# Attention score stages: the last value group at full width, and a reordering of eviction, transposition and stores

## The chip, the cores and the metric

The kernel runs on one NeuronCore of a Trainium2 chip, in one launch. The metric is the device time of a run in microseconds (us); lower is better.

## The reference

Three layers work on x of 2 x 1024 x 128 floats: a mixture-of-experts attention layer added with weight 0.5, a causal multi-query attention layer, and the first layer again. The change touches only the first and the third, which are the same code (phase 0 and phase 1). Cut to what matters, for each batch:

```python
h = layernorm(x)                                   # 1024 tokens, 128 channels
q, k, v = (moe_proj(h, W, b) for W, b in ...)      # gated mix of 4 experts; 16 heads of 8
scores = einsum('bthd,bshd->bhts', q, k) / sqrt(8)
attn = softmax(scores, axis=-1)                    # not causal, all 1024 x 1024
out = einsum('bhts,bshd->bthd', attn, v).reshape(B, T, C)
x = x + 0.5 * (out @ Wo + bo)
```

## The kernel before

**Units.** A unit is one head of one batch; each phase has 32 of them. `it` counts groups of four units and `g` (0 to 3) is the place in the group. The engines run in their own instruction order and meet at semaphores. First iterations and last ones are written out, the middle ones are hardware loops.

**Two score computations.** Softmax needs each query's maximum before the exponentials. For a unit, TensorE computes all scores twice. `max_tile` (L1151) computes 128 queries x 1024 keys in bfloat16, 8 tiles a unit, two units ahead (`AHEAD = 2`), alternating between two pairs of PSUM banks; VectorE reduces each tile to a negated maximum (`maxima`, L912, the reduction at L918). `score_tile` (L1164) computes the transposed scores, 128 keys x 512 queries, 16 tiles a unit, in three banks by `EXP_BANK = [0, 1, 2] * 5 + [1]`; ScalarE takes the exponential of each (`exps`, L765, at L773) into `probs`. The maxima reach the second computation as two extra rows of the stationary operand (50 rows against 48).

**The way of the maxima.** After the 8th reduction GpSimd splits the maxima into two bfloat16 parts (`max_split`, L496 and L498). VectorE transposes them (`max_transpose`, L910), after the reduction of tile 1 of the next unit. SyncE writes them to DRAM (`max_rows_out`, L327) and, once they have landed, reads them back with four small transfers as rows of `stack` (`max_rows_in`, L335). The first score tile of a unit waits for them (L1168).

**Values.** `values` (L1179) multiplies the exponentials of four key tiles (a group `j`) with the values in float32, with a 32-column stationary operand in each of four column groups of the array. Each group is two halves of 256 queries. One instruction of the program is two records in the trace, so a half is 8 records. All results of a pair of units (g = 0 and 1, or 2 and 3) gather in one PSUM bank, `PV_BANK`, so that the bank is evicted once in two units (`evacuate`, L763), on ScalarE. The first group of a new pair waits for that (`o_ready`, L1185).

**Order on TensorE** (`unit`, L1197): for each of 8 steps kt: score tile 2kt, the maximum tile, score tile 2kt+1, then one half of a value group. At kt = 0 and 1 that is the last group (j = 3) of the unit before, and from kt = 2 on it is group kt/2 - 1 of this unit. A half 0 waits until the four exponentials of its group are done (L1187).

**Order on ScalarE**: 16 exponentials; in units with g = 0 or 2 the eviction stands behind the exponential of t = 4.

**Order on SyncE** (body at L364) for each g: `load_stack` of a later unit (waits until all scores of the unit before are done), `max_rows_out`, `store_o` of the evicted pair where g is 0 or 2, `max_rows_in`, and in the last four iterations `load_o`, which reads earlier results back in another layout. One load waits for the store of the same pair. Behind the score loop VectorE normalises (`recip_0` L927, `normalize_1` L933 to L936, which waits for the `load_o` transfers), then adds the output projection (`finish`, L958 and L963).

Of the kernel before, what the change touches and what calls it, by code (L numbers as in the profile page):

```python
# [16 lines left out]
def build(nc, x_in, a_wq, a_wkv, a_null, a_wout, f_wq, f_bq, f_wk, f_bk, f_wv, f_bv,  # L17
          f_wg1, f_bg1, f_wg2, f_bg2, f_wo, f_bo, out):
    B, T, _ = x_in.shape
    NT = T // P  # L20
    HALF = 512
# [5 lines left out]
    NB = 4  # L27
# [12 lines left out]
    with ExitStack() as ctx:  # L40
# [238 lines left out]
        def _(sp):  # L279
# [65 lines left out]
            def ffn(ph):  # L345
                i0 = ph * UNITS // NB
                for b in range(B):
                    store_parts(ph * B + b, b)
                    sp.wait_ge(parts_stored, 16 * 2 * len(PRODUCTS) * (B * ph + b + 1))
                    if b == 0:  # L350
                        sp.wait_ge(stacks_clear, 3 * ph + 1)
                        for g in range(NB):
                            load_stack(g, i0, g)
                max_rows_out(0, i0)
                max_rows_in(0, i0)

                def load_o(n):

                    b, m = n // PAIRS_B, n % PAIRS_B
                    sp.wait_ge(o_stored[n % 2], 16 * (i0 + n // 2 + 1) + 16)  # L360
                    sp.dma_start(o_all[LR * m:LR * m + LR, b].rearrange("p q k c -> p (q k) c"),
                                 o_dram.ap()[n].rearrange("q k r c -> r (q k) c")).then_inc(o_loaded[b], 16)

                def body(i, first, last):  # L364
                    for g in range(NB):
                        after = (i0 + i + 1, 0) if g == NB - 1 else (i0 + i, g + 1)
                        if not (first and g == 0) and not (last and g > 0):
                            load_stack((g - 1) % NB, i0 + i + (1 if g else 0), i * NB + (g + NB - 1))
                        if not (last and g == NB - 1):
                            max_rows_out(after[1], after[0])  # L370
                        if g == 0 and not first:
                            store_o(1, i0 + i - 1, i * 2 - 1)
                        if g == 2:
                            store_o(0, i0 + i, i * 2)
                        if not (last and g == NB - 1):
                            max_rows_in(after[1], after[0])
                        if isinstance(i, int) and HB - 1 <= i <= HB:
                            load_o((i - HB + 1) * NB + g)
                        if isinstance(i, int) and i > HB - 1 and g == 1:
                            load_o(2 * i - 1)  # L380
                        if isinstance(i, int) and i >= HB - 1 and g == 3:
                            load_o(2 * i)
                body(0, True, False)
                with sp.Fori(1, HB - 1) as i:
                    body(i, False, False)
                for i in range(HB - 1, UNITS // NB):
                    body(i, False, i == UNITS // NB - 1)
                store_o(1, i0 + UNITS // NB - 1, UNITS // 2 - 1)
                sp.wait_ge(o_stored[1], 16 * (i0 + UNITS // NB) + 16)
                sp.wait_ge(last_clear, 1)  # L390
                for k in range(4):
                    s = slice((k % 2) * (T // 4), (k % 2 + 1) * (T // 4))
                    sp.dma_start(o_last[32 * k:32 * k + LR, :, :],
                                 o_dram.ap()[UNITS // 2 - 1, k // 2 * 2:k // 2 * 2 + 2].rearrange("a k r c -> r (a k) c")[:, :, s]
                                 ).then_inc(last_loaded, 16)
# [204 lines left out]
        def _(act):  # L600
# [164 lines left out]
            def exps(g, it, first):  # L765

                u = NB * it + g

                for t in range(TB):
                    act.wait_ge(scores_done, TB * u + t + 1)  # L770
                    if t % 4 == 0 and not first:
                        act.wait_ge(pv_done, NT // 2 * u - NT // 2 + t // 4 + 1)
                    nc.scalar.activation(probs[:, t, :], ps[:, EXP_BANK[t], :], ACT.Exp, scale=F_SCALE).then_inc(probs_ready, 1)  # L773
                    if t == 4 and g == 0 and not first:
                        evacuate(1, it - 1)
                    if t == 4 and g == 2:
                        evacuate(0, it)

            def ffn(ph):
# [31 lines left out]
        def _(dve):  # L811
# [100 lines left out]
            def maxima(g, it, first):  # L912

                u = NB * it + g
                for t in range(NT):
                    dve.wait_ge(max_scores, NT * u + t + 1)
                    bank = MAX_BANK[t % 2]
                    nc.vector.tensor_reduce(neg_max[:, g, t:t + 1], ps[:, bank:bank + 2, :].rearrange("p a b -> p (a b)"), AX,  # L918
                                            ALU.max, negate=True).then_inc(max_read, 1)
                    if t == 1 and not first:  # L920
                        max_transpose((g - 1) % NB, it if g else it - 1)

            def recip_0(ph, g):
# [153 lines left out]
            def ffn(ph):  # L1077
# [9 lines left out]
                for g in range(NB):  # L1087
                    maxima(g, i0, g == 0)
# [28 lines left out]
        def _(pe):  # L1117
# [58 lines left out]
                                       stack[rows, g, 0, h * HALF:(h + 1) * HALF], start=True, stop=True)  # L1176
                ins.then_inc(scores_done, 1)

            def values(g, it, j, half):  # L1179

                u = NB * it + g
                if j == 0 and half == 0:
                    pe.wait_ge(v_unit_ready, u + 1)
                    if g % 2 == 0 and not (isinstance(it, int) and 2 * it + g // 2 == 0):
                        pe.wait_ge(o_ready, 2 * it + g // 2)  # L1185
                if half == 0:
                    pe.wait_ge(probs_ready, TB + TB * u + 4 * j + 4)  # L1187
                cols = slice(half * (HALF // 2), (half + 1) * (HALF // 2))
                for t in range(4 * j, 4 * j + 4):
                    row = 32 * (t % 2 * 2 + t // 2 % 2)  # L1190
                    ins = nc.tensor.matmul(ps[row:row + 32, PV_BANK, cols], v_unit[:, g, t // 2, :], probs[:, t, cols],  # L1191
                                           start=j == 0 and half == 0 and g % 2 == 0,
                                           stop=j == NT // 2 - 1 and half == 1 and g % 2 == 1, skip_group_check=True)
                if half == 1:
                    ins.then_inc(pv_done, 1)

            def unit(g, it, first, ahead):  # L1197

                for kt in range(NT):
                    score_tile(g, it, kt, 0)  # L1200
                    if ahead:
                        max_tile((g + AHEAD) % NB, it + (g + AHEAD) // NB, kt)
                    score_tile(g, it, kt, 1)
                    if kt >= 2:
                        values(g, it, kt // 2 - 1, kt % 2)
                    elif not first:
                        values((g - 1) % NB, it if g else it - 1, NT // 2 - 1, kt)

            def finish_0(ph):

# [196 lines left out]
            def ffn(ph):  # L1407
                if ph == 0:
                    norm_T(0, 0)
                    gates(0, 0, 0)  # L1410
                norm_T(2 * ph * B + 1, 1)
                gates(2 * ph * B + 1, ph * B + 1, 1)
                if ph == 0:
                    project(0, 0)
                project(ph * B + 1, 1)
                pe.wait_ge(qkf_ready, 4 * B * (ph + 1))
                pe.wait_ge(v_ready, 2 * B * (ph + 1))
                i0, last = ph * UNITS // NB, (ph + 1) * UNITS // NB - 1
                for g in range(AHEAD):
                    for t in range(NT):  # L1420
                        max_tile(g, i0, t)
                for g in range(NB):
                    unit(g, i0, g == 0, True)
                with pe.Fori(1, UNITS // NB - 1) as i:
                    for g in range(NB):
                        unit(g, i + i0, False, True)
                for g in range(NB):
                    unit(g, last, False, g + AHEAD < NB)
                for half in range(2):
                    values(NB - 1, last, NT // 2 - 1, half)  # L1430
                finish_0(ph)
                if ph == 0:

                    norm_T(B, 0, 5)
                    pe.wait_ge(xnT_ready, 2 * B + 2)
                    queries(0, 0, 0, 0)
                    keys(0)
                finish_1(ph)
                if ph == 0:
                    queries(0, 0, 0, 1)  # L1440
                finish_last(ph)

            ffn(0)
            attention()
            ffn(1)


# [21 lines left out]
```

## Time and profile before

| what | value |
|---|---|
| median of 3 runs | 1426.66 us (1423.76 to 1426.83) |
| the profiled execution, whole | 1426.65 us |
| its span | 1424.9 us |
| TensorE matmul, busy | 1248.4 us, 88% |
| VectorE, busy | 1116.7 us, 78% |
| ScalarE, busy | 930.8 us, 65% |
| GpSimd, busy | 332.6 us, 23% |
| score stage of phase 0 | about 66 to 388 us |
| score stage of phase 1 | about 1092 to 1408 us |

The span is the part of the execution in which the engines' instructions lie; 1.75 us lie around it. A matmul record's end is modelled, and consecutive matmuls overlap, so the starts are what to read on TensorE. "Idle before" in a timeline is followed by the instruction that ended the wait.

### The profile page before, as it was taken

The numbers are of one execution on the slowest core, as the hardware profiler recorded it, in microseconds if no ns is written. First come the engines' busy times: TensorE is split into PE (matmuls) and PEld (weight loads), VectorE is DVE, ScalarE is ACT, GpSimd is POOL, SyncE is SP. The second block draws the span as 40 slices with busy tenths as digits, with TensorE's granted clock in tenths as the row PEclk, the third lists the DMA queues.
The fourth block names the chain that finished last, engine by engine and source line by source line (L and its number), as shares of the span: only waits on it lengthen the run. The fifth ranks groups of instructions, "written<-read, shape, count | busy, mean of one in ns | idle before, by whom it ended". The sixth has DMA issues, their size and how long they took to land. (4 is left out here: it accounts for less than half of the span.)

```text
span 1424.9 us, 32069 instructions
## 1 busy us (share of the span) xinstructions
PE 1248.4 (88%) x10352; PEld 549.4 (39%) x10416; DVE 1116.7 (78%) x1941; ACT 930.8 (65%) x1915; POOL 332.6 (23%) x552
## 2 busy tenths in 40 slices
PE   4599999999947999999999999999867999999896
PEld 2122222222234555555566555555642222222223
DVE  6889899999866766766744766776748999999997
ACT  3289799888826555555543555555423999998894
POOL 4300000002003444444422444443322000000200
PEclk9599899999979999999999999999986999999998
DMA  4512112553122222222220222222042221235422
GB/s 115 189 44 62 49 53 59 94 88 73 32 56 47 47 47 47 46 46 47 47 47 1 47 47 46 46 47 45 1 134 91 61 54 52 57 82 86 82 54 60
DMA packets 58915, 86.59 MB, mean 61 GB/s; under 512 B 22288, under 2 KB 32464, under 8 KB 58832
## 3 DMA queue, kind: packets, MB, share of 16 engines
q1 hardware_dynamic: 58832, 85.53, 25.8%
q8 instruction: 46, 0.75, 0.2%
q14 instruction: 37, 0.30, 0.1%
HBM read 37.79 MB, written 22.54 MB: 42 GB/s over the span
## 5 line engine op out<-in xcount | busy, mean ns | idle before, releaser
L918 DVE TENSOR_REDUCE neg_max<-ps 128x1 f32<-128x1024 f32 x512 | 589.7, 1211 | 41.3 <-PE ps L1160 40.1
L773 ACT ACTIVATE arena<-ps 128x512 f32<-128x512 f32 x1024 | 551.3, 595 | 105.9 <-PE ps L1175 90.5
L1191 PE MATMUL ps<-arena 128*32 128x256 f32 x4096 | 330.9, 395 | 34.5 <-ACT arena L763 32.9
L1175 PE MATMUL ps<-arena 50*128 50x512 bf16 x1024 | 325.4, 389 | 7.8 <-DMA arena<-max_dram 7.7
L1160 PE MATMUL ps<-arena 48*128 48x512 bf16 x1024 | 307.8, 399 | 18.6 <-DVE neg_max L918 16.5
L995 DVE TENSOR_REDUCE a_neg_max<-ps 128x1 f32<-128x129 f32 (+7 forms) x256 | 193.5, 756 | 152.8 <-PE ps L1282 149.4
L576 POOL TENSOR_SCALAR arena<-arena,a_rsum 128x128 f32<-128x128 f32 (+7 forms) x256 | 191.3, 747 | 358.5 <-DVE a_rsum L1003 352.1
L1282 PE MATMUL ps<-arena 128*128 128x512 bf16 (+4 forms) x1280 | 225.6, 301 | 27.6 <-ACT arena L687 18.1
L687 ACT ACTIVATE arena<-ps,a_neg_max 128x129 f32<-128x129 f32 (+7 forms) x256 | 189.8, 741 | 81.0 <-DVE a_neg_max L995 79.4
L697 ACT ACTIVATE arena<-ps 128x128 f32<-128x128 f32 (+1 forms) x192 | 87.1, 454 | 171.3 <-PE ps L1295 169.5
L1295 PE MATMUL ps<-ident,arena 128*128 128x128 f32 x1152 | 172.3, 277 | 14.9 <-DVE arena L1014 14.6
L1282 PEld LDWEIGHTS ps<-arena 128*128 128x128 bf16 x1344 | 110.8, 98 | 165.7 <-issue 59.9
L1191 PEld LDWEIGHTS ps<-arena 128*32 128x32 f32 x4096 | 81.5, 108 | 227.0 <-issue 121.4
L1175 PEld LDWEIGHTS ps<-arena 50*128 50x128 bf16 x1024 | 71.6, 93 | 251.4 <-ACT arena L773 231.0
L1311 PE MATMUL ps<-arena 128*64 128x512 f32 (+3 forms) x768 | 144.2, 498 | 0.8 <-DVE arena L1014 0.7
L1295 PEld LDWEIGHTS ps<-ident,arena 128*128 128x128 f32 x1152 | 122.8, 140 | 25.4 <-DVE arena L1014 8.8
L496 POOL CAST max_parts<-neg_max 128x8 bf16<-128x8 f32 x64 | 12.1, 189 | 498.5 <-DVE neg_max L918 498.5
L1014 DVE COPY arena<-ps 128x512 f32<-128x512 f32 (+1 forms) x192 | 113.9, 593 | 4.9 <-PE ps L1295 3.8
L1311 PEld LDWEIGHTS ps<-arena 128*64 128x64 f32 x768 | 47.5, 136 | 57.7 <-issue 47.9
L1160 PEld LDWEIGHTS ps<-arena 48*128 48x128 bf16 x1024 | 54.7, 94 | 35.9 <-DVE neg_max L918 30.3
L1282 PE MATMUL ps<-causal,ident_bf 128*128 128x128 bf16 (+2 forms) x320 | 61.1, 208 | 0.0
L1005 DVE TENSOR_TENSOR p<-arena,a_rsum 128x1 f32<-128x1 f32 (+1 forms) x256 | 42.8, 167 | 22.9 <-DVE a_rsum L1003 1.5
(120 smaller groups left out, 798.9 us busy)
## 6 DMA issues: line engine op xcount, KB each, us to landing
arena<-stack_dram SPq DMA_DIRECT2D x128, 192.0 KB, 3.5
stack_dram<-arena SPq DMA_DIRECT2D x48, 256.0 KB, 3.9
arena<-arena SPq DMA_DIRECT2D x32, 384.0 KB, 4.2
o_dram<-arena SPq DMA_DIRECT2D x32, 256.0 KB, 2.1
arena<-arena SPq DMA_DIRECT2D x32, 256.0 KB, 5.0
arena<-o_dram SPq DMA_DIRECT2D x30, 256.0 KB, 4.5
arena<-max_dram SPq DMA_DIRECT2D x256, 1.0 KB
arena<-arena SPq DMA_DIRECT2D x32, 128.0 KB, 4.9
```

The source lines that it names most:

```text
L576: nc.gpsimd.tensor_scalar(a_probs[:, t % RING, 1:n], a_probs[:, t % RING, 1:n], a_rsum[:, t:t + 1], 1.0, ALU.mult, ALU.mult).then_inc(a_no ...
L687: nc.scalar.activation(a_probs[:, t % RING, 0:n], ps[:, S_BANK[t % 2]:S_BANK[t % 2] + (n + HALF - 1) // HALF, :].rearrange("p a b -> p (a ...
L773: nc.scalar.activation(probs[:, t, :], ps[:, EXP_BANK[t], :], ACT.Exp, scale=F_SCALE).then_inc(probs_ready, 1)
L918: nc.vector.tensor_reduce(neg_max[:, g, t:t + 1], ps[:, bank:bank + 2, :].rearrange("p a b -> p (a b)"), AX, ALU.max, negate=True).then_in ...
L995: nc.vector.tensor_reduce(a_neg_max[:, t:t + 1], ps[:, S_BANK[t % 2]:S_BANK[t % 2] + (n + HALF - 1) // HALF, :].rearrange("p a b -> p (a b ...
L1014: nc.vector.tensor_copy(probs_T[qh][:, hh, kt:kt + m, (qt % 4) * P:(qt % 4 + 1) * P], ps[:, T_BANK[0], 0:m * P].rearrange("p (k q) -> p k ...
L1160: ins = nc.tensor.matmul(ps[:, bank + h, :], stack[rows, g, 0, t * P:(t + 1) * P], stack[rows, g, 1, h * HALF:(h + 1) * HALF], start=True, ...
L1175: ins = nc.tensor.matmul(ps[:, bank, :], stack[rows, g, 1, kt * P:(kt + 1) * P], stack[rows, g, 0, h * HALF:(h + 1) * HALF], start=True, s ...
L1191: ins = nc.tensor.matmul(ps[row:row + 32, PV_BANK, cols], v_unit[:, g, t // 2, :], probs[:, t, cols], start=j == 0 and half == 0 and g % 2 ...
L1282: ins = nc.tensor.matmul(ps[:, bank, o0:o1], lhs, rhs, start=k == 0, stop=k == len(passes) - 1)
L1295: ins = nc.tensor.transpose(ps[:, T_BANK[use % 2], j * P:(j + 1) * P], a_probs[:, t % RING, 1 + (kt + j) * P:1 + (kt + j + 1) * P], ident[ ...
L1311: ins = nc.tensor.matmul(ps[hh * AD:(hh + 1) * AD, PV_BANK, q0:HALF], av[:, b, kt, :], probs_T[qh][:, hh, kt, q0:HALF], start=kt == 0, sto ...
```

## The change

Four edits, all in the score stages. On TensorE the last value group of a unit is no longer two halves at kt = 0 and 1 of the next unit, but one at 512 columns at kt = 0; kt = 1 has no values. On ScalarE the eviction stands behind the exponential of t = 1, not t = 4. On VectorE the transposition stands behind the first reduction of the next unit, not the second. On SyncE `max_rows_in` comes ahead of `store_o`.

```diff
@@ SyncE, body
                         if not (last and g == NB - 1):
                             max_rows_out(after[1], after[0])
+                        if not (last and g == NB - 1):
+                            max_rows_in(after[1], after[0])
                         if g == 0 and not first:
                             store_o(1, i0 + i - 1, i * 2 - 1)
                         if g == 2:
                             store_o(0, i0 + i, i * 2)
-                        if not (last and g == NB - 1):
-                            max_rows_in(after[1], after[0])
@@ ScalarE, exps
-                    if t == 4 and g == 0 and not first:
+                    if t == 1 and g == 0 and not first:
                         evacuate(1, it - 1)
-                    if t == 4 and g == 2:
+                    if t == 1 and g == 2:
                         evacuate(0, it)
@@ VectorE, maxima
-                    if t == 1 and not first:
+                    if t == 0 and not first:
                         max_transpose((g - 1) % NB, it if g else it - 1)
@@ TensorE, values and unit
-            def values(g, it, j, half):
+            def values(g, it, j, c0, c1):
...
-                cols = slice(half * (HALF // 2), (half + 1) * (HALF // 2))
+                cols = slice(c0, c1)
...
-                        values(g, it, kt // 2 - 1, kt % 2)
-                    elif not first:
-                        values((g - 1) % NB, it if g else it - 1, NT // 2 - 1, kt)
+                        values(g, it, kt // 2 - 1, kt % 2 * (HALF // 2), (kt % 2 + 1) * (HALF // 2))
+                    elif kt == 0 and not first:
+                        values((g - 1) % NB, it if g else it - 1, NT // 2 - 1, 0, HALF)
...
-                for half in range(2):
-                    values(NB - 1, last, NT // 2 - 1, half)
+                values(NB - 1, last, NT // 2 - 1, 0, HALF)
```

## Rows read from the trace of the kernel before

**Rows 1.** Timeline, TensorE, a unit that evicts: start, us, line, what, count [idle <-releaser]

```profile
249.72 0.39 PE L1175 MATMUL ps<-arena 50*128 50x512 bf16 x1
250.25 0.64 PE L1191 MATMUL ps<-arena 128*32 128x256 f32 x8
...
253.65 0.64 PE L1191 MATMUL ps<-arena 128*32 128x256 f32 x8 [1.11 <-ACT arena L763]
254.22 0.39 PE L1175 MATMUL ps<-arena 50*128 50x512 bf16 x1
...
260.00 0.39 PE L1175 MATMUL ps<-arena 50*128 50x512 bf16 x1
```

**Rows 2.** Timeline, ScalarE, the same unit, and the start of the next pair

```profile
250.22 2.81 ACT L773 ACTIVATE arena<-ps 128x512 f32<-128x512 f32 x5 [0.34 <-PE ps L1175]
252.93 0.59 ACT L763 ACTIVATE arena<-ps 128x512 f32<-128x512 f32 x1
...
254.64 5.52 ACT L773 ACTIVATE arena<-ps 128x512 f32<-128x512 f32 x10 [0.63 <-PE ps L1175]
...
269.61 2.81 ACT L773 ACTIVATE arena<-ps 128x512 f32<-128x512 f32 x5 [0.34 <-PE ps L1175]
```

**Rows 3.** Timeline, VectorE and GpSimd, the way of the maxima

```profile
251.12 0.20 POOL L498 TENSOR_TENSOR max_parts<-neg_max,max_parts 128x8 bf16<-128x8 f32 x1 [0.18 <-POOL max_parts L496]
252.67 0.20 DVE L910 STREAM_TRANSPOSE max_T<-max_parts 128x32 bf16<-128x32 bf16 x1
263.03 9.10 DVE L918 TENSOR_REDUCE neg_max<-ps 128x1 f32<-128x1024 f32 x8
```

**Rows 4.** Timeline, end of phase 1: the last two value halves, back to back

```profile
1401.75 5.35 ACT L773 ACTIVATE arena<-ps 128x512 f32<-128x512 f32 x10 [0.16 <-PE ps L1175]
1407.16 1.07 PE L1191 MATMUL ps<-arena 128*32 128x256 f32 x16 [0.20 <-ACT arena L773]
1408.30 0.60 ACT L763 ACTIVATE arena<-ps 128x512 f32<-128x512 f32 x1 [1.19 <-PE ps L1191]
```

**Rows 5.** DMA issues by line: count, KB each, median us from issue to landing

```profile
arena<-stack_dram SPq DMA_DIRECT2D x128, 192.0 KB, 3.5
o_dram<-arena SPq DMA_DIRECT2D x32, 256.0 KB, 2.1
max_dram<-max_T SPq DMA_DIRECT2D x64, 8.0 KB, 1.4
```

**Rows 6.** Timeline, SyncE: maxima written and read back behind two `load_o`

```profile
272.28 0.34 SPq L327 DMA_DIRECT2D max_dram<-max_T  x1
275.90 2.93 SPq L335 DMA_DIRECT2D arena<-max_dram  x4
```

**Rows 7.** Waits between 170 and 1400: who, for whom: total us, times, longest

```profile
PE ps L1175 <- DMA arena<-max_dram: 4.7, 8, 0.9
```

**Rows 8.** Timeline, TensorE: the two long waits for maxima early in phase 0

```profile
89.14 0.39 PE L1175 MATMUL ps<-arena 50*128 50x512 bf16 x1 [1.36 <-DMA arena<-max_dram]
148.67 0.38 PE L1175 MATMUL ps<-arena 50*128 50x512 bf16 x1 [1.32 <-DMA arena<-max_dram]
```

**Rows 9.** Stretches: PE, PEld, DVE, ACT, POOL busy us (x instructions), PEclk, DMA share, GB/s

```profile
149.00:164.00 15.00, 14.10 (x108) 2.89 (x105) 10.12 (x10) 9.61 (x18) 0.37 (x2) 0.66 0.17 47
354.00:374.00 20.00, 18.84 (x196) 5.24 (x194) 18.93 (x17) 18.31 (x35) 1.20 (x5) 1.00 0.15 38
```

**Rows 10.** Timeline, end of phase 0: SyncE's last transfers, and VectorE behind them

```profile
370.29 0.33 SPq L327 DMA_DIRECT2D max_dram<-max_T  x1
...
372.47 2.53 SPq L335 DMA_DIRECT2D arena<-max_dram  x4
375.04 0.44 SPq L361 DMA_DIRECT2D arena<-o_dram  x1
...
379.12 0.69 DVE L933 TENSOR_TENSOR arena<-arena 112x512 f32<-112x512 f32 x1 [2.42 <-DMA arena<-o_dram]
...
392.74 1.65 DVE L830 BATCH_NORM_STATS2 stats<-x 128x6 f32<-128x128 f32 x8
```

More of the change, by code:

```diff
@@ L1177, in score_tile @@
                 ins.then_inc(scores_done, 1)
-            def values(g, it, j, half):
+            def values(g, it, j, c0, c1):
                 u = NB * it + g
-                if j == 0 and half == 0:
+                if j == 0 and c0 == 0:
                     pe.wait_ge(v_unit_ready, u + 1)
@@ L1185, in values @@
                         pe.wait_ge(o_ready, 2 * it + g // 2)
-                if half == 0:
+                if c0 == 0:
                     pe.wait_ge(probs_ready, TB + TB * u + 4 * j + 4)
-                cols = slice(half * (HALF // 2), (half + 1) * (HALF // 2))
+                cols = slice(c0, c1)
                 for t in range(4 * j, 4 * j + 4):
@@ L1191, in values @@
                     ins = nc.tensor.matmul(ps[row:row + 32, PV_BANK, cols], v_unit[:, g, t // 2, :], probs[:, t, cols],
-                                           start=j == 0 and half == 0 and g % 2 == 0,
-                                           stop=j == NT // 2 - 1 and half == 1 and g % 2 == 1, skip_group_check=True)
-                if half == 1:
+                                           start=j == 0 and c0 == 0 and g % 2 == 0,
+                                           stop=j == NT // 2 - 1 and c1 == HALF and g % 2 == 1, skip_group_check=True)
+                if c1 == HALF:
                     ins.then_inc(pv_done, 1)
```

## The prediction

> **What bounds the kernel now.** I read the page's busy shares first and then left them: no engine of the score stages stands out, and a mean says nothing about a wait of 1 us. The timelines of two units do. A pair of units takes 269.61 - 250.22 = 19.39 us [rows 2]: the unit that evicts 260.00 - 249.72 = 10.28 [rows 1], the other 9.11. In the first, TensorE stands 1.11 us ahead of the first value group of the new pair, released by the eviction (L763). That eviction comes late because it stands behind five exponentials: it starts at 252.93, 3.21 us after the unit's first score tile. Behind it ScalarE itself waits 0.63 us for scores that stood behind the blocked values on TensorE [rows 1, 2]. VectorE needs 8 reductions at (9.10 - 1.21)/7 = 1.13, and 0.12 for the transposition, 9.15 a unit or 18.3 a pair [rows 3]. So VectorE is a floor 1.1 us below the pair, and the 9.11 unit has hardly any air on TensorE or VectorE. Everything that follows is a walk along three queues, with T = 0 at a unit's first score tile.
>
> Prices for the walk: a score tile's start to its exponential's start 0.42 (254.22 to 254.64), or 0.50 for the first of a unit (249.72 to 250.22) [rows 1, 2]; an exponential lasts 0.60, and a successor that is not waiting for scores starts 0.49 later (my estimate: the ten in 5.52 us leave a mean of 0.55, of which every second one waits for TensorE) [rows 2]; an exponential's end to a value group that waits for it 0.06 (1407.10 to 1407.16) [rows 4]; a value half to the next score tile 0.57; first score tile to the value half of the same step 0.53 [rows 1].
>
> **The full-width group.** The trace has no 512-column value group. From below and above: two halves back to back last 1.07, and, since a half of 0.64 frees TensorE after 0.57, they take 1.00 [rows 4]; two halves apart take 2 x 0.57 = 1.14 [rows 1]. It streams the same columns as the back-to-back pair, so I take 1.00. That is 0.14 less TensorE work a unit, yet it makes a unit *longer*. Score tile 2 now starts at 0.53 + 1.00 = 1.53 where it started at 0.53 + 0.57 = 1.10. Before, its exponential was just in time; now ScalarE is idle 0.43: exponential 2 starts at 1.95, 3 at 2.45, and ends at 3.05. The unit's own first value half, which waits for exponential 3, starts at 3.11 where it started at 0.53 + 2 x 1.11 = 2.76. (1.11 is a step, 0.53 + 0.57.) After that TensorE and ScalarE alternate as before and nothing is regained. **Cost: 0.35 in each unit without an eviction**; between 0.2, if TensorE catches up where it used to wait 0.23 for exponential 13, and 0.5, if the group takes 1.14.
>
> **The eviction behind exponential 1.** The full group ends at 0.53 + 1.07 = 1.60, and the eviction follows 0.07 later, as 1407.16 + 1.07 = 1408.23 is followed by 1408.30 [rows 4]: start 1.67, where the queue would let it start at 1.49. So ScalarE waits 0.18, a new wait, with all later exponentials queued behind it. Exponential 2 starts at 1.67 + 0.47 = 2.14, 3 at 2.63, and it ends at 3.23. The first value half starts at 3.29. It started at 253.65 - 249.72 = 3.93 [rows 1]. The eviction, done at 2.26, is no longer what it waits for; exponential 3 is. **Gain: 0.64 in each unit that evicts**, new length 9.64. Bounds: 0.3 (the group at 1.14, and the waits on ScalarE not absorbed) to 1.1 (all of the idle time). The pair is then 9.64 + 9.46 = 19.10, still above VectorE's 18.3, which therefore does not take over.
>
> **How often.** In each phase 14 evictions and 15 full groups lie before the last pair; in that pair the two about cancel, since without maximum tiles both units are shorter. That is 2 x (14 x 0.64 - 15 x 0.35) = 2 x (8.96 - 5.25) = **7.4 us gained**.
>
> **The transposition one tile earlier** leaves 1.13 us earlier [rows 3]. Does VectorE wait for GpSimd? GpSimd's second part is done at 251.32, and the new place is 252.67 - 1.13 = 251.54, so 0.2 to spare, and any wait there falls into a gap that the later maximum tile of kt = 1 leaves on VectorE (0.3). Costed at nothing; with a wait of 0.3 more it would cost nothing either, since the pair has 0.8 of air. What it buys: the way to the rows read back is 1.4 to land, 2.5 of issues [rows 5, 10] and another landing. Between 170 and 1400 TensorE waits 4.7 us in 8 places for these rows [rows 7], all but one in the late iterations of a phase, because there the small write lands 3.6 us after its issue (272.28 to 275.90) instead of 1.4 [rows 5, 6]: it stands behind the `load_o` and `load_stack` transfers. An earlier issue alone does not get it past those. But `load_o` follows the rows on SyncE, so the whole train moves forward by about 1.1 us against the next unit. I take back 3.5 of the 4.7; bounds 1 and 6 (the ScalarE and VectorE delays that follow such a wait come on top of TensorE's idle time).
>
> The early two, 1.36 and 1.32 [rows 8], come from writes that landed late for a reason that I do not see in the queue. If the landing follows the issue, 1.13 of each goes; if it is fixed by something else, nothing. I take half, **1.4 us**, bounds 0 and 2.7.
>
> At this place a rule speaks against the move. The Trainium skill ("DMA: Bandwidth & Descriptors", section "Queues, rings and completion order") says that each DMA engine takes the descriptors of one queue in ring order. The earlier write is issued at about 2.0 and the unit's `load_stack`, issued 0.5 to 0.1 before T, lands 3.5 later, at 3.0 to 3.4 [rows 5]. By the rule it lands at about 3.5 and not sooner, which is also 2.0 + 1.4; the sum would stay as it is.
>
> **Stores behind the read back.** SyncE no longer issues the store ahead of the four reads. In the loop this is free: nothing waits for a store within two pairs. At the end of a phase it is not. There the last `load_o` waits for the store of the last pair but one. Today that store goes out before the reads and lands while they are issued; the load follows at 375.04, right behind them, and VectorE, idle 2.42, starts at 379.12 [rows 10]. From there VectorE is busy without a gap until the next stage's statistics at 392.74 [rows 10], so phase 0 ends by this load. After the change the reads start 0.8 earlier, without the store ahead of them (the write goes out at 370.29 and lands 1.4 later, at 371.7, yet they start at 372.47 [rows 5, 10]), they take 2.57 as now, the store takes 2.1 to land [rows 5], and only then the load goes out. The change is 2.1 - 0.8 = **1.3 us lost**, once. In phase 1 the same delay meets a later chain (the last eviction at 1408.30 and its two transfers) with over 2 us of air: nothing. Bounds of the term: 0.5 and 2.
>
> **The clock.** Between 149 and 164 the mean granted clock is 0.66, against 1.00 in quiet stretches, so TensorE was at 1.2 GHz for most of it. It did 108 matmul records, which take 108/9.8 = 11.0 us at the quiet 196 in 20 us: 4.0 us lost [rows 9]. The fall came right after the wait of 1.32 [rows 8]. With that wait shortened and the waits of 1.11 gone (15 in each phase), TensorE pauses less than before, and I expect the fall not to come back: **4.0 gained**.
>
> The Trainium skill ("TensorE: Matmul & The Clock Gate", section "HAM oscillation — how this bites in real kernels") ties a fall to long idle gaps, of which 1.32 us is not one. By it the fall is no consequence of that wait, and need not go with it: 1416 instead of 1412. The rows speak for that as well: the wait of 1.36 before 89.14 was followed by no fall. So this is a rival below, with nearly as much weight.
>
> **Sum**, against the profiled execution's 1426.65 (span 1424.9 plus 1.75), which is also the median, 1426.66: 7.4 + 3.5 + 1.4 - 1.3 + 4.0 = 15.0, giving **1411.7 us**, 1412.
>
> **The rivals.**
>
> *The clock falls anyway* (same mechanism, same place or another): 15.0 - 4.0 = 11.0, 1416. For it: the fall that one wait brought and another did not. Chance 0.30.
>
> *The eviction's slack goes to another wait.* ScalarE is put back 0.54 at exponential 2 in an evicting unit (1.60 to 2.14), and if tiles behind that wait for banks as well, the gain there is 0.3, not 0.64: 28 x 0.34 = 9.5 less, 1421; with the clock's fall 1425. For it: the exponentials' banks leave TensorE only about one tile of lead. Against it: in the walk only the value half waits. Chance 0.13.
>
> *More is gained*: all waits for rows go (6 and 2.7 instead of 3.5 and 1.4), and TensorE makes good 0.15 of the 0.35 at exponential 13: 3.8 + 4.5 = 8 more, 1404. Chance 0.10.
>
> *The full group is dear*: slower than before. If a matmul of 512 columns by four column groups overlaps worse than halves do, each 0.1 above 1.00 costs 0.1 in each of 59 units, 5.9 us. It decides from 1.25 on, where 15 us are eaten. At 1.4 (three serial records of 0.40 and a tail) it is 23.6 lost, 1435. Against it: sixteen halves' records in 1.07 [rows 4]. Chance 0.05.
>
> **How the numbers follow.** Forecast 1412 with 0.42, the others as given. Leaving out the dear group and the outer half of the two rivals beside it gives a range of 1404 to 1422, and the bounds of the unknown terms (rows 1 to 6, tail 0.5 to 2, full group 0.2 to 0.5) lie within it. A difference below 0.2%, 2.9 us, can't be told from none. Faster by more (under 1423.8): the forecast, the clock, more gained, and three quarters of the slack rival, 0.90 less some doubt about the walk, 0.87. Same: 0.08. Slower: 0.05.
>
> **What would show it.** Start to start of first score tiles 9.6 in evicting units and 9.5 in the others. TensorE's waits for L763, 1.1 each before, near zero; instead its values wait for L773, from 3.3. On ScalarE 0.4 idle ahead of exponential 2, or 0.2 ahead of the eviction, released by L1191. Value group to next score tile 1.00. L910 right behind the first reduction, the reads at T + 3.5. VectorE's idle time before L933 in phase 0 3 us or more. The clock at 1.00 from 75 us to the end of the phase. Wrong would be: an evicting unit above 9.9, another above 9.6, or new waits on maxima.

## The result

The changed kernel takes 1418.4 us, median of 9 runs (1416.25 to 1421.17), against 1426.6 for the kernel before, also 9 runs (1423.76 to 1432.69). The ratio is 0.9945, interval 0.9932 to 0.9958, and the medians differ by 8.2 us: faster. The forecast was 1412 with a range of 1404 to 1422. The sign and the range held, and a bit more than half of the 15 us came.

The profiled execution took 1417.99, which is 8.7 under that of before. The page's first lines of the kernel after:

```profile
span 1416.3 us, 31045 instructions
PE 1256.9 (89%) x9840; PEld 550.5 (39%) x9904; DVE 1121.9 (79%) x1941; ACT 929.2 (66%) x1915; POOL 334.0 (24%) x552
```

As before, the shares say nothing of what was gained. The unit that evicts does, beside [rows 1]. TensorE in the kernel after (start, us, line, what, count, idle before and its releaser):

```profile
242.20 0.39 PE L1175 MATMUL ps<-arena 50*128 50x512 bf16 x1
...
242.74 1.07 PE L1191 MATMUL ps<-arena 128*32 128x512 f32 x8
243.74 0.39 PE L1175 MATMUL ps<-arena 50*128 50x512 bf16 x1
...
245.09 0.39 PE L1175 MATMUL ps<-arena 50*128 50x512 bf16 x1 [0.31 <-ACT arena L773]
245.58 0.64 PE L1191 MATMUL ps<-arena 128*32 128x256 f32 x8
246.15 0.39 PE L1175 MATMUL ps<-arena 50*128 50x512 bf16 x1
...
251.93 0.39 PE L1175 MATMUL ps<-arena 50*128 50x512 bf16 x1
```

With T = 242.20, the full-width group holds TensorE for 243.74 - 242.74 = 1.00, and the first value half of the unit starts at 245.58, T + 3.38, where it started at T + 3.93. The wait of 1.11 for L763 is gone. This unit is 251.93 - 242.20 = 9.73 long (9.65 in every second pair) against 10.28.

ScalarE in the same pair, beside [rows 2]:

```profile
242.71 1.08 ACT L773 ACTIVATE arena<-ps 128x512 f32<-128x512 f32 x2 [0.34 <-PE ps L1175]
243.95 0.60 ACT L763 ACTIVATE arena<-ps 128x512 f32<-128x512 f32 x1 [0.15 <-PE ps L1191]
244.44 7.65 ACT L773 ACTIVATE arena<-ps 128x512 f32<-128x512 f32 x14
252.43 1.08 ACT L773 ACTIVATE arena<-ps 128x512 f32<-128x512 f32 x2 [0.34 <-PE ps L1175]
253.89 7.65 ACT L773 ACTIVATE arena<-ps 128x512 f32<-128x512 f32 x14 [0.37 <-PE ps L1175]
261.88 1.08 ACT L773 ACTIVATE arena<-ps 128x512 f32<-128x512 f32 x2 [0.34 <-PE ps L1175]
```

Two exponentials, 0.15 of waiting for the full group, the eviction, and then 14 exponentials without a wait that shows. In the unit that does not evict, 0.37 of idle time stands in the eviction's place. The pair takes 261.88 - 242.71 = 19.17 (before 19.39).

VectorE: the transposition is right behind the first reduction and does not wait for GpSimd; the later maximum tile leaves 0.19 behind it, as an idle time and not as a delay.

```profile
243.99 0.20 DVE L910 STREAM_TRANSPOSE max_T<-max_parts 128x32 bf16<-128x32 bf16 x1
244.38 9.42 DVE L918 TENSOR_REDUCE neg_max<-ps 128x1 f32<-128x1024 f32 x8 [0.19 <-PE ps L1160]
```

The clock where it had been 0.66 [rows 9], and SyncE and VectorE at the end of phase 0, beside [rows 10]:

```profile
149.00:164.00 15.00, 14.53 (x143) 3.80 (x145) 14.78 (x14) 13.89 (x27) 0.63 (x3) 1.00 0.18 54
```

```profile
363.94 2.57 SPq L335 DMA_DIRECT2D arena<-max_dram  x4
366.55 0.44 SPq L342 DMA_DIRECT2D o_dram<-arena  x1
368.69 0.35 SPq L361 DMA_DIRECT2D arena<-o_dram  x1
...
372.77 0.69 DVE L933 TENSOR_TENSOR arena<-arena 112x512 f32<-112x512 f32 x1 [3.84 <-DMA arena<-o_dram]
```

The clock is at 1.00. In the tail the load now waits for the store, 2.14 behind it, and VectorE is idle 3.84 ahead of L933 instead of 2.42.

**Where the 8.7 us are**, by the starts of the first score tiles of all units in the two profiled executions:

| term of the sum | predicted | measured |
|---|---|---|
| steady units (evicting 10.28 to 9.65 and 9.73; others 9.11 to 9.45, 9.54 outside the hardware loop) | 7.4 | 5.8 |
| late waits for rows: what units 20 to 25 and 52 to 57 take above their quiet length, 6.0 before, 7.1 after | 3.5 | -1.1 |
| the two early waits [rows 8] (units 1 and 7: 10.54 and 10.49 to 9.54 and 9.44; the 0.8 that both lose as units without an eviction stands in the first line) | 1.4 | 2.8 |
| clock (unit 8: 14.39 to 9.65, of which 0.6 counts as steady) | 4.0 | 4.1 |
| tail of phase 0 | -1.3 | -1.3 |
| first units of both phases (0.68 and 0.46 longer), start, attention stage (everything between the two score stages), end | none | -1.7 |
| sum | 15.0 | 8.6 |

The one term with the wrong sign is the late waits; 4.6 of the 6.3 missing us are there. Most experiments below are about it and about which of the edits earns what.

### The profile page after: what moved, and what is told of

Read it like the earlier page. It is cut to its first block and busy times, and to the rows that moved or that the text cites. A ratio compares the mean times of both kernels' runs of the same rounds, so it can differ in the third digit from the quotient of the medians.

```text
span 1416.3 us, 31045 instructions
## 1 busy us (share of the span) xinstructions
PE 1256.9 (89%) x9840; PEld 550.5 (39%) x9904; DVE 1121.9 (79%) x1941; ACT 929.2 (66%) x1915; POOL 334.0 (24%) x552
## 5 line engine op out<-in xcount | busy, mean ns | idle before, releaser
L773 ACT ACTIVATE arena<-ps 128x512 f32<-128x512 f32 x1024 | 545.6, 597 | 92.9 <-PE ps L1175 80.8
L1191 PE MATMUL ps<-arena 128*32 128x256 f32 (+1 forms) x3584 | 316.5, 425 | 8.5 <-ACT arena L773 3.1
L1160 PE MATMUL ps<-arena 48*128 48x512 bf16 x1024 | 297.5, 397 | 19.1 <-DVE neg_max L918 17.0
L1191 PEld LDWEIGHTS ps<-arena 128*32 128x32 f32 x3584 | 71.1, 108 | 165.2 <-issue 90.5
L1160 PEld LDWEIGHTS ps<-arena 48*128 48x128 bf16 x1024 | 57.8, 94 | 41.4 <-DVE neg_max L918 30.4
L1282 PE MATMUL ps<-causal,ident_bf 128*128 128x128 bf16 (+2 forms) x320 | 61.1, 208 | 0.0
```

The source lines that it names most:

```text
L1160: ins = nc.tensor.matmul(ps[:, bank + h, :], stack[rows, g, 0, t * P:(t + 1) * P], stack[rows, g, 1, h * HALF:(h + 1) * HALF], start=True, ...
L1282: ins = nc.tensor.matmul(ps[:, bank, o0:o1], lhs, rhs, start=k == 0, stop=k == len(passes) - 1)
```

## The experiments

Each was timed against the kernel before on the same chip. "Quiet" units are those without a wait for rows. A "fall" is a stretch in which the granted clock is 0.50, that is 1.2 GHz, within a score stage. Unit lengths and falls are read from one profiled execution of each kernel.

**1. The full-width group alone**, in the kernel before:

```diff
-    elif not first:
-        values((g - 1) % NB, it if g else it - 1, NT // 2 - 1, kt)
+    elif kt == 0 and not first:
+        values((g - 1) % NB, it if g else it - 1, NT // 2 - 1, 0, HALF)
```

> The kernel before with only the full-width value group. My theory: the group holds the next score tile back by 0.43 us, and since the eviction still stands behind exponential 4, both units get longer: the unit without an eviction 9.11 to 9.46, the evicting one 10.28 to about 10.5 (first value half at T + 4.14 in place of 3.93). Pair 19.95, 28 pairs x 0.56 = 16 us over before, about 1441 in all. The rival, that less TensorE work per unit (0.14 us) is worth something by itself, expects 1422 to 1427.

Measured: 1452.2 us, ratio 1.0186 (1.0167 to 1.0206), 26 us slower. Units 9.45 and 10.50: the pair is 19.95, as worked out. The 11 us more than expected are for the most part clock. TensorE, an evicting unit, and the stretches about it (busy us and instructions of PE, PEld, DVE, ACT, POOL, then the granted clock, DMA share, GB/s):

```profile
192.13 0.39 PE L1175 MATMUL ps<-arena 50*128 50x512 bf16 x1
193.68 0.64 PE L1191 MATMUL ps<-arena 128*32 128x256 f32 x8 [1.16 <-ACT arena L763]
194.25 0.56 PE L1175 MATMUL ps<-arena 50*128 50x512 bf16 x1
```

```profile
193.00:194.00 1.00, 0.32 (x8) 0.16 (x8) 1.00 (x2) 1.00 (x3) 0.00 (x0) 1.00 0.05 5
194.00:195.00 1.00, 1.00 (x12) 0.11 (x4) 0.15 (x1) 0.19 (x2) 0.00 (x0) 0.67 0.42 147
195.00:196.00 1.00, 1.00 (x10) 0.20 (x8) 0.72 (x1) 0.93 (x2) 0.00 (x0) 0.50 0.32 119
196.00:197.00 1.00, 1.00 (x8) 0.13 (x4) 0.50 (x1) 0.09 (x1) 0.00 (x0) 0.50 0.02 2
```

A wait of 1.16 for the eviction, and TensorE goes on at 0.50, 1.2 GHz; this unit is 12.03 long, not 10.50. It happens seven times in the score stages, for 3.41 us each; at 1.53 each that is 10.7 us. The one fall of the kernel before, which had cost 4.1, is not there, so the clock makes 6.6 of the difference. Another 3.2 lie in the attention stage, whose code is the same (703.0 us against 699.8, from L830 behind phase 0 to the first score tile of phase 1). So the full group by itself costs 0.35 in a unit without an eviction, as the prediction says, and 0.22 in one with it.

**2. The early eviction with two halves**: the changed kernel, but for the halves.

```diff
-    elif kt == 0 and not first:
-        values((g - 1) % NB, it if g else it - 1, NT // 2 - 1, 0, HALF)
+    elif not first:
+        values((g - 1) % NB, it if g else it - 1, NT // 2 - 1, kt * (HALF // 2), (kt + 1) * (HALF // 2))
```

> The changed kernel with the last value group in two halves again, the eviction still behind exponential 1. My theory: the second half ends at T + 2.3, so ScalarE waits 0.9 us for it with all exponentials queued behind, the first value half comes at T + 3.98, as late as before the change (3.93); the other unit is back at 9.11. Pair 19.44 against 19.14 measured after, 28 x 0.3 = 8 us over the changed kernel, 1426. The rival, that the early eviction alone makes the gain and the full-width group only costs 0.35 per unit, expects 8.81 to 9.11 in units without eviction, 9.65 in evicting ones, and 1408 to 1412.

Measured: 1429.1, ratio 1.0011 (0.9997 to 1.0025). Quiet units 9.11 and 10.33 to 10.41. It has two falls of 3.4 us, one in the last pair of each phase, behind waits of 0.97. TensorE and ScalarE, an evicting unit with T = 204.72:

```profile
208.29 0.39 PE L1175 MATMUL ps<-arena 50*128 50x512 bf16 x1 [0.75 <-ACT arena L773]
208.78 0.64 PE L1191 MATMUL ps<-arena 128*32 128x256 f32 x8
```

```profile
207.15 0.60 ACT L763 ACTIVATE arena<-ps 128x512 f32<-128x512 f32 x1 [0.83 <-PE ps L1191]
```

The second half ends at T + 2.28, so the eviction holds all of ScalarE 0.83 there, and the first value half starts at T + 4.06, not 3.38. Neither of the two edits is good alone: the full group without the early eviction costs 26 us, the early eviction without the full group gains nothing, though this kernel has the early transposition as well. Together they gain 0.6 in an evicting unit and lose 0.35 in the other: 0.25 a pair (19.39 to 19.14).

**3. The store ahead of the read back**, as it was:

```diff
-    if not (last and g == NB - 1):
-        max_rows_in(after[1], after[0])
     if g == 0 and not first:
         store_o(1, i0 + i - 1, i * 2 - 1)
     if g == 2:
         store_o(0, i0 + i, i * 2)
+    if not (last and g == NB - 1):
+        max_rows_in(after[1], after[0])
```

> The changed kernel with the store of the pair ahead of the read back again. My theory: VectorE's wait for the last load at the end of phase 0 falls by 1.3 us (its first normalisation at 10.7 instead of 12.0 us after the first score tile of the last pair), and in the late iterations the store no longer lengthens the train of transfers; 1 to 3 us below the changed kernel, 1416. The rival, that the order of these two does not matter, expects the same time and the normalisation at 12.0.

Measured: 1417.9, ratio 0.994 (0.9922 to 0.9958), not to be told from the changed kernel. In the trace the tail is right: from the first score tile of phase 0's last pair to the next stage's statistics (L830) it takes 24.47, against 25.63 in the changed kernel. The 1.2 us are there, below what the totals resolve. Its late units take 2.5 us less than the changed kernel's in these two traces (table below): 1.1 less in phase 0, where neither has a fall, and 1.4 in phase 1, where the changed kernel has one. The prediction had called the new place of the store free in the loop. The totals do not show either gain; in these two executions the attention stage took 702.6 us and 700.0, which hides most of it.

**4. The late loads one a unit.** In the changed kernel three units of each phase issue two `load_o`. Here each late unit issues at most one, and the three loads taken out go into later units:

```diff
-    if isinstance(i, int) and i > HB - 1 and g == 1:
-        load_o(2 * i - 1)
-    if isinstance(i, int) and i >= HB - 1 and g == 3:
-        load_o(2 * i)
+    if isinstance(i, int) and i == HB + 1:
+        load_o(8 + g)
+    if isinstance(i, int) and i == HB + 2 and g != 2:
+        load_o((12, 13, 0, 14)[g])
```

> The changed kernel with the loads of earlier results one per unit in the late iterations, where it issues two in three of the units. My theory: the late waits for maxima are a closed loop of transfers: read back, two loads, two stack loads, and only then the next small write lands. Without the doubled loads the write lands about 3.5 us after its issue at most, and the units 22 to 25 and 54 to 57 of the trace, 7.1 us over the quiet ones in all, fall to 1 us over; 6 us less, 1412. The rival, that the small write is late for some other reason than the loads queued ahead of it, expects 1418 and the excess unchanged.

Measured: 1411.1, ratio 0.99 (0.988 to 0.992), 7.3 us under the changed kernel. No late unit is longer than a quiet one, and no wait for rows is left between 66 and 1410. SyncE in the changed kernel, and TensorE waiting for it:

```profile
299.78 0.92 SPq L361 DMA_DIRECT2D arena<-o_dram  x2
300.74 0.89 SPq L318 DMA_DIRECT2D arena<-stack_dram  x2
303.19 0.34 SPq L327 DMA_DIRECT2D max_dram<-max_T  x1
308.63 2.57 SPq L335 DMA_DIRECT2D arena<-max_dram  x4
```

```profile
312.74 0.38 PE L1175 MATMUL ps<-arena 50*128 50x512 bf16 x1 [1.64 <-DMA arena<-max_dram]
```

and its issues between 299 and 309 (count, KB each, median us from issue to landing):

```profile
arena<-o_dram SPq DMA_DIRECT2D x2, 256.0 KB, 5.5
arena<-stack_dram SPq DMA_DIRECT2D x2, 192.0 KB, 7.0
...
max_dram<-max_T SPq DMA_DIRECT2D x1, 8.0 KB, 5.4
```

The 8 KB write takes 5.4 us instead of 1.4: it lands at 308.61, 0.17 behind the second stack load (308.44). So it goes for all writes of units 20 to 24 in both phases: nine of the ten land 0.16 to 0.19 behind the second stack load ahead of them, one 0.53. From one landing to the next but one it takes 20.7 to 21.1 us, where a quiet pair takes 19.2. The Trainium skill ("DMA: Bandwidth & Descriptors", section "Queues, rings and completion order") has descriptors of one queue taken in ring order on each DMA engine; this trace agrees. With the loads spread, SyncE of that kernel:

```profile
300.48 0.34 SPq L327 DMA_DIRECT2D max_dram<-max_T  x1
301.92 2.56 SPq L335 DMA_DIRECT2D arena<-max_dram  x4
...
305.02 0.43 SPq L361 DMA_DIRECT2D arena<-o_dram  x1
307.64 0.80 SPq L318 DMA_DIRECT2D arena<-stack_dram  x2
```

The write is followed by the reads 1.44 later, and the four reads, one load and two stack loads repeat in 9.6 us.

**5. The eviction in other places, with halves.** Two kernels, experiment 2 with `t == 3` and with `t == 2` in place of `t == 1` in `exps`.

> The changed kernel with the last value group in two halves and the eviction behind exponential 3. My theory: the second half ends at T + 2.3, exponential 3 lets go at 2.52, so the eviction waits for nothing and is read at 3.2; the first value half starts at T + 3.24 in place of 3.38 (changed kernel) or 3.93 (before), and the other unit is back at 9.11. Pair 9.11 + 9.6 = 18.7 against 19.14: 28 x 0.44 = 12 us under the changed kernel, 1406, with the late waits for maxima as large or larger. The rival, that VectorE or the way of the maxima takes over below 19 us a pair, expects 18.9 to 19.1 and idle time on TensorE released by L918 or by the maxima's read back, 1414 or more.

> The same with the eviction behind exponential 2. My theory: ScalarE waits 0.33 us for the second half, exponential 3 ends at T + 3.43 and the first value half comes at 3.49: pair 18.95, 7 us over half_evac3. If the first value half waited for the eviction alone, it would come at 3.1 and the pair would be 18.6.

Measured: 1410.5, ratio 0.9888 (0.9865 to 0.9911), and 1416.9, ratio 0.9933 (0.9912 to 0.9955). Quiet units 9.11 and 9.59, and 9.11 and 9.84 to 9.92: pairs of 18.70 and 18.99, both below the changed kernel's 19.14 on average. With the eviction behind the 4th exponential (T = 201.34), ScalarE and TensorE:

```profile
203.84 0.60 ACT L763 ACTIVATE arena<-ps 128x512 f32<-128x512 f32 x1
```

```profile
204.58 0.64 PE L1191 MATMUL ps<-arena 128*32 128x256 f32 x8 [0.41 <-ACT arena L763]
```

The eviction no longer waits for TensorE, since the second half is done by then (it ends at T + 2.3 and the eviction starts at T + 2.50), and the first value half waits for it only 0.41 and starts at T + 3.24, earlier than the 3.38 of the changed kernel; no unit pays the 0.35 of the full group. Behind the 3rd exponential (`t == 2`) the eviction goes ahead of exponential 4 (t = 3), for which the value group waits, so TensorE waits for L773 there (22.5 us in 34 waits, longest 0.9), and the unit is 0.3 longer. The total with `t == 3` missed its expectation by 4 us: its late units again take 11.5 us above their quiet length, against 7.1 in the changed kernel, with one fall of 6.8 us among them.

**6. The transposition late**, in the changed kernel: `if t == 1 and not first:` in `maxima` instead of `t == 0`.

> The changed kernel with the transposition behind the second reduction again. The maxima are then ready at about T + 9.0 to 9.4 of a 9.45 us unit. If the earlier transposition is what removed the two early waits of 1.3 and 1.4 us and the fall of the clock behind the second, some of them return: 1420 to 1425, with waits of L1175 for the read back in units before the 20th. If it did nothing, 1418.

Measured: 1429.9, ratio 1.0016 (0.9998 to 1.0033): 11.5 us slower than the changed kernel by the medians (10 by the ratios), more than any theory had. The quiet units are 9.45 and 9.65 to 9.73 as before; what is added is waits. Between 66 and 1410 (total us, times, longest), this kernel and then the changed one:

```profile
PE ps L1175 <- DMA arena<-max_dram: 13.3, 13, 1.6
PEld ps L1175 <- DMA arena<-max_dram: 5.7, 5, 1.7
```

```profile
PE ps L1175 <- DMA arena<-max_dram: 4.7, 4, 1.7
```

Two of these waits, 1.52 and 1.21, are followed by a fall of 3.4 us (units 21 and 57). The write goes out at T + 3.55, where it went out at T + 3.14 in the kernel before and at T + 2.01 in the changed one. In a quiet unit it lands 1.42 later, the four reads take 2.57 and the last of them lands about 1.8 later (1.78 in the kernel before): T + 9.3 of a unit of 9.45. That is an estimate from these rows; the same sum gives T + 8.9 of 9.11 before and T + 7.9 of 9.45 in the changed kernel.

**7. The transposition alone**, in the kernel before: `t == 0` in `maxima`, nothing else.

> The kernel before with only the transposition moved behind the first reduction. If the earlier transposition has a worth of its own, the two early waits for maxima go and 1.13 us of slack come in each unit: 3 to 7 us below before, 1420 to 1423, the late waits about as before. If it only pays for the slack that the shorter units of the changed kernel took away (late_transpose lost 11.5 us without it), the time stays within 2 us of before.

Measured: 1420.1, ratio 0.9973 (0.9962 to 0.9984), 4.6 us faster on its chip by the medians (3.9 by the ratio). Its profiled execution, 1417.84, is the fastest of the seven, so its trace shows more than the median gained. Units 1 and 7 are 9.11 long, unit 8 is 10.28 and not 14.39, and the clock is at 1.00 from 149 to 164 there too. The late units take 2.7 us less than in the kernel before.

**8. The best parts together**: experiment 5 with `t == 3`, the loads of experiment 4, the stores ahead of the reads. And the same with the stores behind the reads.

> half_evac3 with the loads of earlier results one per unit and the stores ahead of the read back. My theory: 18.7 us a pair also in the late iterations, and 1.3 us less at the end of phase 0: 8 to 9 us below half_evac3, 1397. If the late waits come from the small write's own latency, they stay and it is 1404.

> The fastest version so far (two halves, eviction behind exponential 3, loads one per unit) with the stores behind the read back, as the changed kernel has them. My theory: the order costs at the end of phase 0 alone, where VectorE's first statistics come 25.6 us after the first score tile of the last pair in place of 23.8: 1 to 2 us slower, 1400, with all units as before. The rival, that the store in the train of transfers also lengthens late units, expects units of the last four iterations above 9.11 and 9.59, and 1402 or more.

Measured: 1398.3, ratio 0.98 (0.9777 to 0.9823), and 1398.8, ratio 0.9813 (0.98 to 0.9826). Every unit from the second to the last but two of a phase is 9.11 or 9.59. From the phase's last pair to L830 it is 23.78 against 25.67: the stores' place is again seen in the tail and not in the totals, and in these two executions the attention stage differs the other way, 702.8 and 700.3. A stretch of 100 us of the first:

```profile
200.00:300.00 100.00, 97.53 (x1030) 25.76 (x1024) 98.67 (x98) 93.37 (x178) 6.94 (x33) 1.00 0.33 81
```

VectorE is busy 98.7% of it, TensorE 97.5%. The floor of 18.3 us a pair that [rows 3] gave is now 0.4 away.

**What six late units take.** Units 20 to 25 and 52 to 57, beside three quiet pairs of the same kernel:

| kernel | quiet | 20 to 25 | 52 to 57 |
|---|---|---|---|
| before | 58.2 | 60.6 | 61.7 |
| transposition alone | 58.2 | 60.2 | 59.4 |
| full group alone | 59.9 | 60.9 | 62.5 |
| changed | 57.4 | 60.9 | 61.0 |
| changed, stores ahead | 57.4 | 59.9 | 59.6 |
| halves, eviction t = 1 | 58.4 | 60.6 | 61.9 |
| halves, eviction t = 3 | 56.1 | 61.6 | 62.1 |
| halves, eviction t = 2 | 57.0 | 60.6 | 61.1 |
| changed, late transposition | 57.4 | 63.8 | 64.1 |
| changed, loads spread | 57.4 | 57.4 | 57.4 |
| best, either place of the stores | 56.1 | 56.1 | 56.1 |

Each row is one trace. Falls lie within the late units of the full group alone, the changed kernel, the halves with t = 3 (all one, 52 to 57), the halves with t = 2 and the late transposition (one in each block).

## Why the prediction was right in sign and short in size

**The walk along the queues held** (mechanism and term right). Group 1.00, predicted 1.00; ScalarE's new wait 0.15, predicted 0.18; first value half at T + 3.38, and T + 3.10 without an eviction, predicted 3.29 and 3.11; units 9.45 as against 9.46. Mis-sized was the evicting unit's gain: 9.64 was predicted and met in every second pair, the other is 9.73; and units outside the hardware loop cost 0.42 instead of 0.35. That is the 1.6 between 7.4 and 5.8. The rival "the eviction's slack goes to another wait" did not come (9.98 it would have been), nor did the dear group: each 512-column group is exactly what two halves back to back were [rows 4].

**The late waits: the step that failed.** The prediction said that `load_o` follows the rows on SyncE, "so the whole train moves forward by about 1.1 us against the next unit", and took 3.5 us back; 1.1 were lost. The traces take the 4.6 between them apart, by the lengths of the twelve late units against twelve quiet ones:

- The transposition alone brings the waits from 6.0 to 3.3. That is 2.7 of the 3.5.
- With the units shortened as well, stores ahead, they are 4.6. The late units are as long as with the transposition alone (119.5 against 119.6 us), so of the 1.5 that the engines saved there by the quiet lengths 1.3 went into waiting. The prediction counted that saving in the 7.4 and did not take it off here.
- With the stores behind the reads they are 7.1. The prediction had the store as free in the loop, but in the late units it stands between the reads and the next loads. One fall of the clock is in these 2.5 us.

What these units are paced by is a closed train: the write lands when the loads ahead of it have landed, then the reads go out, then the next `load_o` and stack loads, and the next write stands behind those. In the six kernels with the early transposition and doubled loads the quiet length goes from 58.4 down to 56.1, and the blocks keep to 59.4 to 62.1, in no order with it.

Once each write lands right behind the loads, to issue it earlier does not shorten the round, and a shorter unit only turns more of the round into waiting. Experiment 4 takes the second load out of three units a phase, and the block falls to its quiet length. With the late transposition the train is not closed in every unit: the kernel before and the changed kernel with it lose in the late units, and there the earlier write gains, 2.7 and 5.9 us.

The clause on an "earlier issue alone" in the prediction was right for units with two loads ahead of the write; the gain behind it holds only until the train is closed. By hindsight the term is about 60.6 minus the new quiet length for each block: 2 x (60.6 - 57.4) = 6.4 of waits to remain, and 7.1 was measured. The prediction itself had named new waits on maxima as a sign of being wrong, and here they came.

**The early waits** went wholly, 2.8 for 1.4: I had taken half between two bounds, and the upper bound was right. Experiment 7 shows that the transposition alone does it. Why those two writes took 3.1 and 3.5 us to land in the kernel before was not found. Such landings have not gone away: one early write takes 2.8 us in the changed kernel and one 3.1 with the transposition alone. The earlier issue leaves enough time that no score tile waits for them.

**The clock** came back, 4.1 for 4.0, and the rival of a fall elsewhere got its say in small: one fall of 3.4 us at 1312, in a late unit with a wait for rows. Experiment 7 took only the two early waits away and left all waits of 1.11, and the fall at 150 was gone. Experiment 1, with waits of 1.16 in evicting units, had seven falls. Other kernels here had one or two, in late units or in the last pair. Of the 16 falls in the score stages of the twelve traces, 15 begin 0.1 to 1.5 us behind the end of a TensorE wait of 0.97 to 1.69 us, and one as a wait of 1.73 ends. But the 30 waits of 1.11 with the transposition alone brought none. So that a fall follows such a wait is what the traces show; which wait brings it they do not settle, and that the wait of 1.32 brought the fall at 150 is not proven.

**The tail** was right: -1.3 for -1.3, VectorE idle 3.84 for "3 us or more". Experiments 3 and 8 show it at 1.2 and 1.9.

**The transposition** was costed at nothing and given 4.9 us of gains in rows. As "nothing on VectorE" it was right. What was not seen is that it is the edit on which the others stand: it is worth 4.6 us in the kernel before and 11.5 in the changed one. In the quiet units it makes no difference in either. With the late transposition in the changed kernel the write also goes out 0.4 later in its unit, and the evicting units are 0.6 shorter; the time left is used up in the late units and in some early ones (10.80 and 10.95 for 9.45 to 9.73).

**Not foreseen**: the first unit of each phase is 0.7 and 0.5 longer. Why is not shown; over the twelve traces the first unit of phase 1 took 11.15 to 13.14 us. The rest, 0.5, is in the start, the attention stage and the end. The attention stage, the same code in all kernels, took 699.8 to 700.3 us in five profiled executions and 702.2 to 703.5 in seven. In the five the granted clock is 0.50 for 61.9 to 68.2 us of the stage, in the seven for 70.8 to 75.5; the two go together, which comes first is not shown. So differences of a few us between single totals rest on unit lengths here, not on totals.

**The chances**: with three quarters of the slack rival they add up to 0.92, not 0.90; nothing hangs on it.

## What to carry to other kernels

When a small transfer that someone waits for shares a queue with large ones, work out the round of the queue and compare it with the loop. While the round is longer, a faster loop gains nothing there, and an earlier issue gains only until the small transfer stands right behind the large ones; spreading the large transfers evenly gained all of it here. Whatever else stands in that train, a store too, is not free. An eviction belongs behind the operation after which its input is complete anyway, and not ahead of one that the next stage waits for; here that was two places later than the change put it, and it made the wider group unnecessary. Shortening a loop uses up the slack of everything timed against it, so an edit that moves such a thing forward can be worth 4.6 us alone and 11.5 beside the others, without any quiet unit showing it.

## What was not expected of the hardware

- TensorE's clock fell to 1.2 GHz behind waits of 1.12 to 1.16 us in experiment 1, seven times, each for 3.41 us by the records. The Trainium skill ("TensorE: Matmul & The Clock Gate", section "HAM oscillation — how this bites in real kernels") ties falls to long idle gaps; this trace has them without one (the waits ahead of its falls are 1.12 to 1.16 us).
- A value group of 512 columns in four column groups takes 1.00 from its start to the next tile, a half of 256 takes 0.57. Two halves apart pay 0.14 more, yet gave the shorter pair, because the tile behind the wide group comes 0.43 later.
- An 8 KB write took 5.4 us to land behind two loads of 256 KB and two of 192 KB, and 1.4 with one load and two stack loads issued at other times.
